# Layer 1's projections and expert up-products: full 32-bit matmuls replaced by three one-pass matmuls of high and low parts

## The reference

```python
# layer 1, mixer: 16 key heads, 32 value heads of 128
qkv = xn @ W_qkv.T            # 8192 columns: q, k, v
z = xn @ W_z.T                # 4096 columns, the gate
beta, dt = sigmoid(xn @ W_b.T), softplus(xn @ W_a.T + dt_bias)
qkv = conv_over_time(qkv, conv_w, taps=4)
# per token: state = decay*state + k (v - k.state)*beta ; o = q.state
y = (rmsnorm(o) * silu(z)) @ W_out.T
# layer 1, experts: 2 shared + 16 routed (top 2), 256 -> 128 -> 256
h = gelu(xn @ W_up[e]);  f += gate[e] * (h @ W_down[e])
out = x + y * silu(f)
```

## Time and profile before

| | |
|---|---|
| median of 3 runs | 1662.02 us (1661.52 to 1663.77) |
| the profiled execution: its time, its span | 1661.06 us, 1659.3 us |
| granted TensorE clock, mean of full speed | 0.961 |
| busy: PE, PEld, DVE, ACT, POOL | 91%, 67%, 72%, 59%, 33% |
| layer 1's first gate product starts at | 317.8 us |

### The profile page before, as it was taken

How to read it: one execution, slowest core, us unless ns; L and a number is a source line. 1 busy time by engine, 2 the same in 40 slices (tenths; PEclk the granted TensorE clock), 3 DMA queues, 4 the chain that set the end, 5 groups by cost and what they waited for, 6 DMA issues and landing times.

```text
span 1659.3 us, 31971 instructions
## 1 busy us (share of the span) xinstructions
PE 1515.7 (91%) x11984; PEld 1116.9 (67%) x11984; DVE 1201.2 (72%) x2605; ACT 973.2 (59%) x2524; POOL 541.1 (33%) x674
## 2 busy tenths in 40 slices
PE   6998777799999999999999998999999999999984
PEld 3554323547777777778777777787878686777873
DVE  3467424477888777788877787878797978787773
ACT  2100343176766667677676767676867575767663
POOL 6000022325343233334333333333434232433223
PEclk9999777799999999999999999999999999999997
DMA  9920000121010111110101010110102010100000
GB/s 282 116 38 4 4 1 1 51 44 44 27 33 26 34 28 31 33 39 20 40 14 46 19 40 21 39 39 27 39 20 46 14 46 18 36 20 21 1 2 26
DMA packets 52736, 59.26 MB, mean 36 GB/s; under 512 B 5352, under 2 KB 45032, under 8 KB 52584
## 3 DMA queue, kind: packets, MB, share of 16 engines
q1 hardware_dynamic: 52584, 57.23, 15.0%
HBM read 51.71 MB, written 5.51 MB: 34 GB/s over the span
## 4 chain that ended last, share of the span: by engine, by line
PE 49%; DVE 9%; ACT 6%; DMA 4%; POOL 4%; issue 2%; SPq 0%; POOLq 0%; DVEq 0%; ACTq 0%
PE ps L913 10%; PE ps L1091 6%; PE ps L948 4%; DMA RC<-crow 4%; PE ps L957 2%; PE ps L1069 2%; PE ps L965 2%; PE ps L1073 2%; PE ps L1061 2%; PE ps L997 2%; PE ps L1007 2%; PE ps L1045 2%; PE ps L1010 2%; PE ps L1081 2%; DVE QC L1338 1%
## 5 line engine op out<-in xcount | busy, mean ns | idle before, releaser
L1652 ACT ACTIVATE XY<-ps 128x512 f16<-128x512 f32 x384 | 220.3, 605 | 101.9 <-PE ps L1010 100.4
L1771 POOL TENSOR_TENSOR RC<-RC,dec 128x512 f32<-128x512 f32 x64 | 66.9, 1046 | 325.1 <-DMA RC<-crow 325.1
L1403 DVE TENSOR_TENSOR ZL<-ps,cst 128x256 f16<-128x256 f32 x384 | 153.2, 416 | 24.4 <-PE ps L997 23.8
L1338 DVE SCALAR_TENSOR_TENSOR yv<-ps,cw,yv 128x511 f32<-128x511 f32 (+2 forms) x192 | 143.2, 746 | 9.5 <-ACT yv L1591 5.0
L1091 PE MATMUL ps<-WO,OGT 128*128 128x256 f32 x512 | 129.0, 397 | 4.4 <-ACT OGT L1691 3.3
L913 PE MATMUL ps<-xnT,WK 128*128 128x512 f32 x256 | 126.3, 618 | 4.1 <-DVE QC L1338 1.5
L948 PE MATMUL ps<-WV,xnT 128*128 128x256 f32 x512 | 126.5, 390 | 1.4 <-DVE O L1458 0.7
L913 PE MATMUL ps<-xnT,WV 128*128 128x512 f32 x256 | 124.2, 608 | 0.0
L1091 PEld LDWEIGHTS ps<-WO,OGT 128*128 128x128 f32 x512 | 97.0, 196 | 24.3 <-ACT OGT L1691 6.1
L1684 ACT ACTIVATE sq<-O 128x128 f32<-128x128 f32 x256 | 79.3, 310 | 51.0 <-DVE O L1458 20.5
L1470 DVE SCALAR_TENSOR_TENSOR O<-O,small,Z 128x128 f32<-128x128 f32 x256 | 81.7, 381 | 37.4 <-POOL small L1802 37.4
(11 more groups left out here) (225 smaller groups left out, 3969.3 us busy)
## 6 DMA issues: line engine op xcount, KB each, us to landing
RC<-crow SPq DMA_DIRECT2D x128, 128.0 KB, 3.9
WV<-in_WV SPq DMA_DIRECT2D x16, 512.0 KB, 3.6
WK<-in_WK SPq DMA_DIRECT2D x16, 256.0 KB, 2.7
WO<-in_WO SPq DMA_DIRECT2D x16, 256.0 KB, 3.1
KS<-spread SPq DMA_DIRECT2D x6, 512.0 KB, 17.8
QS<-spread SPq DMA_DIRECT2D x6, 512.0 KB, 41.7
up<-in_up SPq DMA_DIRECT2D x18, 128.0 KB, 2.2
dn_w<-in_down SPq DMA_DIRECT2D x18, 128.0 KB, 2.4
```

The costliest lines, as they stand in the source:

```text
L1338: m = dve.scalar_tensor_tensor(out=dst[:, k:512], in0=ps[:, bk, 0:512 - k], scalar=cw[:, h, j, 3 - k:4 - k], in1=dst[:, k:512], op0=ALU.mu ...
L1403: leave(dve.tensor_tensor(half(ZL[:, k - 2], k, 0), p, lv(k), ALU.mult), "a", u, k)
L1652: leave(act.activation(changed(u, k), ps[:, bank("b", u, k), :].rearrange("p (c n t) -> p c n t", c=2, t=1 << (k - 1)), ACT.Copy), "b", u, k)
```

## The change

A 32-bit float `x` is written as a high part in TensorE's one-pass 32-bit format (`F32R`) and a low part `x - high`. A product is then three one-pass matmuls into the same PSUM tile: high x high, high x low, low x high. Before, it was one full 32-bit matmul.

- `XH`, `XL` take the place of `xnT` in layer 1. `XH` is written where `xnT` was (VectorE for tiles 0 to 3, ScalarE for 4 to 7); VectorE makes every `XL` by a subtraction. TensorE enters layer 1 after the last `XL`.
- GpSimd splits every weight tile after its fetch: a copy to the high part, a subtraction to the low part, which is written over the fetched tile. In `ORDER1` these are new parts of `fWK`, `fWV` and `fup` on GpSimd. The first two `WK` and the small `wr` and `wab` are split during layer 0.
- `RCS` goes from 3 to 2, so that the new tiles find room.
- Costs and dependences of the planner follow, so the order changes.

```diff
-RCS = 3
+RCS = 2
...
-    P.add(("rt1",), -9, ("PE", 3.6), ("DVE", 0.3), takes=True, gives=("rt1",))
-    P.add(("wab",), -9, ("PE", 3.6), takes=True)
+    P.add(("rt1",), -9, ("PE", 5.4), ("DVE", 0.3), takes=True, gives=("rt1",))
+    P.add(("wab",), -9, ("PE", 5.4), takes=True)
...
-        P.add(x, rank[k], ("PE", 1.72, (("fWK", h), "SP") if h > 1 else None), ("ACT", 0.69, to), ("DVE", 2.25),
+        P.add(x, rank[k], ("PE", 1.3, (("fWK", h), "POOL")), ("ACT", 0.69, to), ("DVE", 2.25),
...
-            P.add(x, rank[6 + 4 * q + b], ("PE", 1.72, wv), ("ACT", 0.6, to), ("DVE", 0.69), takes=True, gives=x)
+            P.add(x, rank[6 + 4 * q + b], ("PE", 1.35, wv), ("ACT", 0.6, to), ("DVE", 0.69), takes=True, gives=x)
...
-    P.add(("fWK", h + 2), 4 * h, ("SP", 3.0, (("cq", h, 0), "PE"), (("cq", h, 1), "PE")))
+    P.add(("fWK", h + 2), 4 * h, ("SP", 3.0, (("cq", h, 0), "PE"), (("cq", h, 1), "PE")), ("POOL", 1.9))
...
-    P.add(("fWV", h + 2), 4 * h, ("SP", 4.5, *values))
+    P.add(("fWV", h + 2), 4 * h, ("SP", 4.5, *values), ("POOL", 3.8))
...
+            def three(o, wh, wl, xh, xl, c, turned=False):
+
+                for k, (a, b) in enumerate(((wh, xh), (wh, xl), (wl, xh))):
+                    if turned:
+                        a, b = b, a
+                    m = pe.matmul(o, a, b, start=c + k == 0, stop=c == 1 and k == 2)
+                return m
...
-                    w.wait_ge(d_wt[h % 2], 16 * (h // 2 + 1))
+                    wh, wl, s_wt, k0, _, _ = conv_tile(x)
+                    bk = enter(*x)
+                    w.wait_ge(s_wt, h + 1)
                     for c in range(2):
-                        m = pe.matmul(ps[:, bk, :], wt[:, h % 2, c, k0:k0 + 128], xnT[:, c, 512 * b:512 * b + 512],
-                                      start=c == 0, stop=c == 1)
+                        at = slice(512 * b, 512 * b + 512)
+                        m = three(ps[:, bk, :], wh[:, h % 2, c, k0:k0 + 128],
+                                  wl[:, h % 2, c, k0:k0 + 128], XH[:, c, at], XL[:, c, at], c)
...
+                    w.wait_ge(s_xh, n + 1)
+                    leave(dve.tensor_tensor(XL[:, :, at], turned, XH[:, :, at].bitcast(F32), ALU.subtract), *x)
...
+            def split(raw, hi, lo, s_hi, s_lo, n):
+
+                pool.tensor_copy(hi, raw).then_inc(s_hi, 1)
+                w.wait_ge(s_hi, n)
+                pool.tensor_tensor(lo, raw, hi.bitcast(F32), ALU.subtract).then_inc(s_lo, 1)
+
+            def split_WV(h):
+                w.wait_ge(d_WV[h % 2], 16 * (h // 2 + 1))
+                split(WV[:, h % 2], WVh[:, h % 2], WVl[:, h % 2], s_hWV, s_sWV, h + 1)
```

More of the change, by code:

```diff
@@ L326, in plan_expert @@
                   takes=True, gives=x)
-    P.add(("fup", e + 2), rank, ("SP", 3.0, *[(("dn", e, b, q), "PE") for b in range(2) for q in range(2)]))
+    if e < 16:
+        P.add(("fup", e + 2), rank, ("SP", 3.0, *[(("dn", e, b, q), "PE") for b in range(2) for q in range(2)]),
+              ("POOL", 1.0))
 def order1():
@@ L332, in order1 @@
     plan_prologue(P)
+    for h in range(2):
+        P.add(("fWV", h), -8 + 4 * h, ("POOL", 3.8))
+        P.add(("fup", h), -7 + 4 * h, ("POOL", 1.0))
+        P.add(("fWK", h), -20 + h, ("POOL", 0.01))
     for h in range(HK):
@@ L466, in room, with twins @@
             return [(s_free[b], n) for b, n in BANKS.prior[key]]
+        def twins(first, second, shape):
+            here = ExitStack()
+            a = sb(first, shape, scope=here)
+            here.close()
+            return a, sb(second, shape, F32R)
         cst = sb("cst", [128, C_END])
         xt = sb("xt", [128, NT, D])
-        xnT = sb("xnT", [128, 2, 1024])
+        xnT, XH = twins("xnT", "XH", [128, 2, 1024])
+        XL = sb("XL", [128, 2, 1024], F32R)
         st = sb("st", [128, NT, D])
@@ L480, in build @@
         iota = cst[:, C_IO:C_IO + 16]
-        wr = sb("wr", [128, 2, 16])
-        wab = sb("wab", [128, 2, 64])
+        wr, wrl = twins("wr", "wrl", [128, 2, 16])
+        wab, wabl = twins("wab", "wabl", [128, 2, 64])
         rows = sb("rows", [128, 64])
@@ L737, in run_sync @@
                     fetch(WO, "WO", h, d_WO)
-                elif what == "fup" and h < 18:
+                elif what == "fup":
                     for b in range(2):
@@ L766, in signal, with gate_logits1 @@
                 m.then_inc(full(*key)[0], 1)
+            def three(o, wh, wl, xh, xl, c, turned=False):
[4 more added lines that the diff above has]
+                return m
+            def gate_logits1(key, wh, wl, E_):
+                bk = enter(*key)
+                for n in range(NT):
+                    at = slice(128 * n, 128 * n + 128)
+                    for c in range(2):
+                        m = three(ps[:, bk, E_ * n:E_ * n + E_], wh[:, c], wl[:, c], XH[:, c, at],
+                                  XL[:, c, at], c, turned=True)
+                signal(m, *key)
             def gate_logits(key, wt, E_):
@@ L890, in run_tensor @@
                 if what == "rt1":
-                    gate_logits(x, wr, 16)
+                    w.wait_ge(s_gs, 2)
+                    gate_logits1(x, wrh, wrl, 16)
                 elif what == "wab":
-                    gate_logits(x, wab, 64)
+                    w.wait_ge(s_gs, 2)
+                    gate_logits1(x, wabh, wabl, 64)
                 elif what == "cum":
@@ L944, in run_tensor @@
                     bk = enter(*x)
-                    w.wait_ge(d_WV[h % 2], 16 * (h // 2 + 1))
+                    w.wait_ge(s_sWV, h + 1)
                     for k in range(2):
+                        at = slice(128 * (n + k), 128 * (n + k) + 128)
                         for c in range(2):
-                            m = pe.matmul(ps[:, bk, 256 * k:256 * k + 256],
-                                          xnT[:, c, 128 * (n + k):128 * (n + k) + 128], WV[:, h % 2, c, 256:512],
-                                          start=c == 0, stop=c == 1)
+                            m = three(ps[:, bk, 256 * k:256 * k + 256], WVh[:, h % 2, c, 256:512],
+                                      WVl[:, h % 2, c, 256:512], XH[:, c, at], XL[:, c, at], c,
+                                      turned=True)
                     signal(m, *x)
@@ L954, in run_tensor @@
                     bk = enter(*x)
-                    w.wait_ge(d_up[e % 2], 32 * (e // 2 + 1))
+                    w.wait_ge(s_sup, e + 1)
                     for c in range(2):
-                        m = pe.matmul(ps[:, bk, :], up[:, e % 2, c, :], xnT[:, c, 512 * b:512 * b + 512],
-                                      start=c == 0, stop=c == 1)
+                        at = slice(512 * b, 512 * b + 512)
+                        m = three(ps[:, bk, :], uph[:, e % 2, c], upl[:, e % 2, c], XH[:, c, at],
+                                  XL[:, c, at], c)
                     signal(m, *x)
@@ L1500, in run_scalar @@
             for n in range(NT):
-                take_turned(0, n)
+                take_turned(n)
             w.wait_ge(d_qk, 32)
@@ L1549, in run_scalar @@
                 elif x[0] == "ln1" and x[1] > 3:
-                    take_turned(1, x[1])
+                    n = x[1]
+                    w.wait_ge(*full(*x))
+                    w.wait_ge(s_xh, n)
+                    act.activation(XH[:, :, 128 * n:128 * n + 128],
+                                   ps[:, bank(*x), 0:256].rearrange("p (c t) -> p c t", c=2), ACT.Copy).then_inc(s_xh, 1)
             def v3(a):
@@ L1804, in run_gpsimd @@
                     scale_wo(x[1])
+                elif x[0] == "fWK" and x[1] > 1:
+                    split_WK(x[1])
+                elif x[0] == "fWV":
+                    split_WV(x[1])
+                elif x[0] == "fup":
+                    split_up(x[1])
             for n in range(NT):
```

62 lines of the change are left out of this document (41 added, 21 removed).

## The result

The changed kernel takes 1686.12 us (median of 4 runs, 1682.97 to 1689.21), against 1662.89 us (1661.52 to 1664.79) for the kernel before on the same chip: the ratio is 1.0139, with a 95% interval of [1.0112, 1.0166]. It is slower by 1.4%, 23 us. The prediction said 55 us faster, with a range that ended at 1642 us.

A forecast was written before the change was run, and what follows sets the result against it. The prediction took TensorE's stream as the bound, with VectorE behind it. Its terms, -65.5 - 5 + 6.5 + 5 + 4 = -55 us, gave 1607 us, with a range for all cases of 1572 to 1642 us.

The forecast's parts named there:

- The step that failed: Layer 1's path: claimed it can only lose the products' -65.5 us, a new order perhaps up to 87 us.
- the other three: Rivals: splits delaying GpSimd's order, 1647 us (12%); late rows, +96 or +192 us (8%); unhidden weight loads, some 1760 us (3%).
- The products' term: Shorter large products and gate pieces on TensorE's path after 412 us: 49.8 plus 15.7 us saved, -65.5 us.
- the -5 us before 412 us: Half of the 10.5 us saved by 20 large products and 4 `Zt` standing before 412 us; bounds 0 and -10.5 us.
- The bounds (1.29 to 2.70 us): Limits for one large three-pass product on TensorE, taken at 1.35 us; 2.70 us means no gain from the format.
- The gates: `wr` and `wab` products at layer 1's start: 48 load-bound matmuls each, plus the last `XL`, +6.5 us; bounds +3.5 and +7.
- GpSimd's splits: Weight splits on GpSimd: 91 us of work costing +5 us, and 75 us of waiting for fetches costing +4 us.
- Two row buffers: Two buffers for fetched rows in place of three: taken to cost nothing, since a unit outlasts a row's way.
- The slower rival by the rows: Row fetches come late with two buffers, GpSimd's `RC` waits well over 400 us: +96 us (1703 us) or +192 us; chance 8%.
- Work counts: First rival: the remade order keeps TensorE at its 95% fill, so all saved work counts, 1571 us; chance 19%.
- Open loads: Rival: the new format's weight loads do not run beside TensorE's matmuls, `Zt` takes 2.65 us, some 1760 us; chance 3%.

The follow-up runs named there:

- e2: e1 with the planner's product costs lowered to 1.3 and 1.35 us, so only the order changes: 1666.3 us, ratio 1.0035.
- e1: Kernel before, its order and three row buffers kept, with three one-pass matmuls per product reading a fixed weight tile, no splits: 1628.2 us, ratio 0.9819.
- e7: Complete changed kernel with the planner's old costs, 1.72 us for products and 3.6 us for gates: 1636.4 us, ratio 0.9860.
- e5: Kernel before, full-precision products, with the changed kernel's costs (1.3 and 1.35 us) in its planner: 1716.4 us, ratio 1.0334.
- e14: e13 with the products of e1, order the same on every engine, nothing split: 1611.8 us, ratio 0.9692.
- e3: Changed kernel in its own order, GpSimd's splits replaced by tiny signalling operations, products reading a fixed tile: 1677.8 us, ratio 1.0099.
- e6: Kernel before with two row buffers in place of three, the order remade for that: 1659.8 us, ratio 0.9989.
- e4: Changed kernel with only the high x high matmul of each product, the two correction passes left out: 1636.8 us, ratio 0.9856.
- e9: Complete changed kernel with 1.66 us in the planner's table for large products and gate pieces: 1642.3 us, ratio 0.9874.
- e10: Complete changed kernel with 2.0 us in the planner's table for large products and gate pieces: 1634.0 us, ratio 0.9845.
- e12: Kernel before, full-precision products kept, with 2.0 in place of 1.72 us in the planner's table: 1646.1 us, ratio 0.9914.
- e11: Complete changed kernel, planner's product costs 1.49 us and its delay behind TensorE parts 0.45 in place of 0.22 us: 1620.8 us, ratio 0.9757.
- e13: Kernel before, products and costs kept, with the planner's delay behind TensorE parts 0.45 in place of 0.22 us: 1654.8 us, ratio 0.9931.
- e15: Complete changed kernel, planner's product costs 1.49 us and its delay behind TensorE parts 0.70 us: 1637.9 us, ratio 0.9843.

## Why the prediction was wrong

**The step that failed** is the sentence "With the order kept, the path that is there keeps all its VectorE, ScalarE, GpSimd and transfer pieces and can only lose this; a new order may do better, up to the 87 us". The order was not kept, and the new one was taken as harmless or better. It costs 36 us on the same products (e2 - e1), 46 us in the changed kernel (against e7) and 56 us in the kernel before (e5). No rival had this mechanism: the first expected the new order to help, the other three looked for slower splits, rows or loads, and the forecast went wrong by the order in which unchanged engines were asked. The diff showed the cause plainly: it wrote 1.3 us for a product that the prediction itself put at 1.35 us and that takes 1.49 us, in a table whose old entry, 1.72, stood under a measured 1.80 us by much less.

**The products' term**, -65.5 us, was mis-sized. Their work fell by 60.5 us and not by 87: 512 columns take 0.233 us and not 0.225, the first matmul behind other work has 0.1 us more, and a `Zt` is 1.49 and not 1.36 us. By the prediction's own proportion that makes 65.5 x 60.5 / 87 = -46 us on the path, and the -5 us before 412 us, also all products, become -3 or -4: -49 us. Measured for both together were -30 us (e1) and -40 us (e14); the part before 412 us was not measured apart. The rest, 9 to 19 us, was not on the path once it was shorter; that the chain of before loses what its pieces lose is an upper bound, since a chain of another engine takes over. The mechanism was right: a chunk's three matmuls of 0.233 us take the place of two instructions of 0.45 us. The bounds (1.29 to 2.70 us) held.

**The gates**, +6.5 us: 20.5 us against 13.7, +6.8 in place of 6, since the clock stayed at 0.50 to their end, where the prediction had the last dozen at full clock. `XL` costs 1.2 us in place of some 0.4: from TensorE's last turns of `xn` to the first gate matmul it is 319.20 - 314.46 = 4.74 us, against 317.83 - 314.25 = 3.58 us before.

**GpSimd's splits**, +5 and +4 us: 6.6 us in e3, with GpSimd 97 us less busy there. That fits, though the uncertainty of 7 us doesn't say more than that the term is small, and each subtraction was dearer than the 1.05 us taken. GpSimd in the changed kernel, grouped by line:

```profile
L1767 POOL TENSOR_TENSOR WVl<-WV,WVh 128x1024 fp32r<-128x1024 f32 x16 | 37.9, 2366 | 1.3
L1767 POOL TENSOR_TENSOR WKl<-WK,WKh 128x512 fp32r<-128x512 f32 x16 | 20.4, 1275 | 1.3
...
L1765 POOL CAST WKh<-WK 128x512 fp32r<-128x512 f32 x16 | 9.9, 617 | 94.6 <-DMA WK<-in_WK 94.6
```

Waits for a fetch ahead of a split were 94.6 + 16.4 + 23.9 us for `WK`, `WV` and `up`, not 75 us, and the waits for `RC` fell by 54 us in return.

**Two row buffers** at nothing: -2 us, within what can be told from no change (e6). The slower rival by the rows is refuted with it: it had `RC` waits well over 400 us, and they are 271 us.

**The other rivals.** Work counts: e1, e4 and e14 refute it, since a fifth (e4) to six tenths (e14) of the work taken from TensorE comes through. Open loads: refuted by 0.117 us from start to start in `Zt`, 1.49 us in place of 2.65.

**What it forecast of the profile.** TensorE's idle time was to rise by 30 us and rose by 59 us; its busy time in 400 to 1600 us was to fall by 90 us and fell by 51 us; VectorE at 80% instead of 83%; GpSimd busy for 104 us more, not 91. Both of TensorE's numbers were off towards a slower kernel.

**The sum by parts measured**: -30 (e1) + 36 (order) + 6.8 (gates) + 1.2 (`XL`) + 6.6 (splits) - 2 (rows) = +19 us, against +23 us. The 4 us left are within the sum of the intervals.

**What stays open.** That the order is the cause is shown (e2, e5, e7). That thin cover is how it costs is supported: by e9, e10 and e12, which were forecast from it, and by the waits at `a` and `ot`, which hold 28 of the 59 us of new idle time in the changed kernel, but only 11 of 36 us in e5. Some of the wait at `ot` is a slow `on`, as at 701 us, and how much was not measured. e11, e13 and e15 lie 5 to 15 us off the count, and whether the harm is done in TensorE's own order or in those of ScalarE and VectorE, which the planner draws at the same time, was not told apart. Of the order's cost about a third is longer busy time (12.7 of 36.7 us in e2, 18 of 54 us in e5, 15 of 46 us in the changed kernel against e7); by its size the lower granted clock accounts for all of it in e2, for most of it in e5 and for some 6 us in the third pair (estimates), and the rest is open.

## What to carry to other kernels

Where a planner draws the order from a table of costs, an edit of the table is an edit of the kernel, and often the larger one: price it apart from the work, by running the old instructions in the new order and the new ones in the old. Here a cost that was too short was much worse than one that was too long, and the reason that fits is that it takes away the work that hides the steps between engines; measure new instructions before writing their cost down, and try a planner's delay as well. A chain of which an engine holds half gives back at most the part that is on it, and here 45% to 60% of the work saved in the products.
